# Reordering the fills of a tile in a fused attention kernel: score block first, maximum block second, bias fill ahead of the sums

## The reference

```
x = x + attention(group_norm(x))        # 32 groups, no learned scale
qkv = gn @ qkv_w + qkv_b                # 12 heads of 16 channels, S = 2304 positions
attn = softmax(q k^T / 4 + rel_h[.., row of key] + rel_w[.., column of key])
out = (attn @ v) @ proj_w + proj_b
```

## Time and profile before

| | |
|---|---|
| runs | 6806.47, 6808.59, 6817.65 us; median 6808.59 us |
| profiled execution, first to last instruction | 6801.4 us (no run time of its own was noted for it) |
| TensorE clock granted, mean | 0.996 |
| busy PE / DVE / ACT / POOL | 99% / 80% / 70% / 14% |

### The profile page before, as it was taken

The page is one execution under the profiler, slowest core; times in us unless marked ns, Lnnn a source line. Parts: engine busy times, 40 slices in busy tenths (PEclk is TensorE's granted clock), DMA queues, the critical chain, the costliest instruction groups (busy, mean ns, idle before and its releaser), DMA issues.

```text
span 6801.4 us, 139326 instructions
## 1 busy us (share of the span) xinstructions
PE 6725.5 (99%) x53600; PEld 4245.8 (62%) x53600; DVE 5454.7 (80%) x9973; ACT 4753.7 (70%) x10225; POOL 938.1 (14%) x967
## 2 busy tenths in 40 slices
PE   7999999999999999999999999999999999999998
PEld 5666666666666666666665666666666666666664
DVE  7887888778887788877888778887888878888883
ACT  3776776767767777677776767767676676767775
POOL 2111010211112110121111210102101121101110
PEclk8999999999999999999999999999999999999999
DMA  6676676767677677667676766767677676777673
GB/s 164 148 156 152 137 160 138 163 151 142 152 144 168 144 143 156 149 158 149 142 155 149 158 143 143 161 145 166 140 144 157 147 165 138 143 152 156 144 154 88
DMA packets 306307, 1013.72 MB, mean 149 GB/s; under 512 B 107440, under 2 KB 196976, under 8 KB 215920
## 3 DMA queue, kind: packets, MB, share of 16 engines
q1 hardware_dynamic: 305648, 1004.81, 68.9%
HBM read 745.26 MB, written 255.69 MB: 147 GB/s over the span
## 4 chain that ended last, share of the span: by engine, by line
PE 96%; DMA 1%; DVE 1%; issue 0%; ACT 0%; SPq 0%; POOL 0%; DVEq 0%; ACTq 0%
PE work L805 30%; PE work L878 27%; PE work L796 27%; PE work L824 7%; PE work L843 3%; PE work L862 2%; PE work L851 1%; DMA moving<-rel_scratch 1%; DVE mpart L683 1%; PE work L830 0%; DVE xb L674 0%; ACT probs L561 0%; DMA back<-attention_scratch 0%; DVE hi L721 0%; PE work L835 0%
## 5 line engine op out<-in xcount | busy, mean ns | idle before, releaser
L683 DVE TENSOR_REDUCE mpart<-work 128x1 f32<-128x512 f32 (+1 forms) x8640 | 5088.7, 632 | 1079.7 <-PE work L805 1013.1
L561 ACT ACTIVATE probs<-work 128x512 f32<-128x512 f32 (+1 forms) x8640 | 4100.2, 564 | 866.6 <-PE work L796 852.1
L805 PE MATMUL work<-mkeys,hi 128*128 128x512 f32 (+1 forms) x8640 | 3404.1, 395 | 10.6 <-DVE mpart L683 8.8
L796 PE MATMUL work<-moving,keys 113*128 113x512 f32 (+1 forms) x8640 | 3299.9, 383 | 10.9 <-DMA moving<-rel_scratch 5.7
L805 PEld LDWEIGHTS work<-mkeys,hi 128*128 128x128 f32 x8640 | 1643.6, 190 | 622.4 <-DVE mpart L683 324.0
L878 PE MATMUL work<-probs,vall 128*17 128x288 f32 x27648 | 2013.1, 409 | 0.0
L796 PEld LDWEIGHTS work<-moving,keys 113*128 113x128 f32 x8640 | 1642.1, 190 | 362.3 <-ACT probs L561 39.2
L878 PEld LDWEIGHTS work<-probs,vall 128*17 128x17 f32 x27648 | 637.3, 96 | 846.8 <-ACT probs L561 358.3
L824 PEld LDWEIGHTS work<-image,tab 128*48 128x48 f32 x6912 | 401.6, 124 | 544.9 <-ACT probs L561 513.2
L490 POOL TENSOR_TENSOR full<-full,hi 128x384 f32<-128x384 f32 x576 | 583.5, 1016 | 938.7 <-DVE hi L721 937.6
L495 POOL TENSOR_TENSOR rden<-oraw,rden 128x576 f32<-128x576 f32 x96 | 137.1, 1428 | 3955.3 <-DMA rden<-inverse_scratch 3955.3
(11 more groups left out here) (42 smaller groups left out, 646.8 us busy)
## 6 DMA issues: line engine op xcount, KB each, us to landing
moving<-rel_scratch SPq DMA_DIRECT2D x1728, 144.0 KB
moving<-qk_scratch SPq DMA_DIRECT2D x288, 576.0 KB
rel_scratch<-hi SPq DMA_DIRECT2D x192, 432.0 KB, 5.7
rel_scratch<-full SPq DMA_DIRECT2D x192, 432.0 KB, 5.5
moving<-rel_scratch SPq DMA_DIRECT2D x288, 288.0 KB
image<-qk_scratch SPq DMA_DIRECT2D x384, 144.0 KB, 3.2
keys<-qk_scratch SPq DMA_DIRECT2D x192, 288.0 KB, 7.8
qk_scratch<-split_hi SPq DMA_DIRECT2D x144, 192.0 KB, 3.9
```

Of the source, the lines that this page charges most:

```text
L561: act.activation(probs[:, tile % RING, lo:up], bank[:, 0:up - lo], ACT.Exp).then_inc(act_read, 1)
L683: dve.tensor_reduce(mpart[:, u % 2, q, m:m + 1], bank[:, 0:MSPLIT[m][1] - MSPLIT[m][0]], AX.X, ALU.max)\
L796: pe.matmul(bank[:, 0:up - lo], tile_of(keys[0:K_ROWS, u % 2, :], c, third), moving[0:K_ROWS, slot_of(u, third)[0], lo:up], start=True, st ...
L805: pe.matmul(bank[:, 0:up - lo], hi[:, u % 2, q * P:(q + 1) * P], mkeys[:, u % 2, lo:up], start=True, stop=True).then_inc(for_dve, 1)
```

## The change

The score block goes ahead of the plan's items of a step. The score order becomes short block first, the maximum order short block last. The bias fill goes from the head of step 0 to step 5, where the items now go ahead of the sums. ACT's order and the numbering in `counts()` follow. No instruction is added or removed. One tile's order on PE is then: score(256) max(512) score(512) max score max score max score(512) max(256) [rel], then the sums.

```diff
-SPLIT = [(512 * i, min(512 * i + 512, N)) for i in range(5)]
+MSPLIT = [(512 * i, min(512 * i + 512, N)) for i in range(5)]
+SPLIT = MSPLIT[-1:] + MSPLIT[:-1]
 SB = len(SPLIT)
-MSPLIT = SPLIT[-1:] + SPLIT[:-1]
...
             if t < 12 and u + 2 < UNITS:
-                plan[u][t][0].insert(0, ("rel", u + 2, t))
+                plan[u][t][SB].append(("rel", u + 2, t))
...
                 if 0 <= u < UNITS and i < SB:
-                    items.append(("score", TILES * u + t, i))
+                    items.insert(0, ("score", TILES * u + t, i))
...
                     for i in range(SB + 1):
+                        if 0 <= u < UNITS and i < SB:
+                            consume(("score", TILES * u + t, i))
                         for item in plan[u][t][i]:
                             if item[0] in ON_ACT:
                                 consume(item)
-                        if 0 <= u < UNITS and i < SB:
-                            consume(("score", TILES * u + t, i))
...
                     for i in range(SB + 1):
+                        if 0 <= u < UNITS and i < SB:
+                            fill(("score", tile, i))
+                        for item in plan[u][t][i]:
+                            fill(item)
                         if i == SB and 0 < tile <= TILES * UNITS:
                             attend(tile - 1)
-                        for item in plan[u][t][i]:
-                            fill(item)
-                        if 0 <= u < UNITS and i < SB:
-                            fill(("score", tile, i))
```

## The result

The changed kernel took 6832.66 us (median of 6 runs, 6829.57 to 6834.45) against 6811.73 us for the kernel before in the same runs: a ratio of 1.003, 95% interval 1.0019 to 1.0041. So it is 0.3% slower, 21 us by the medians. The forecast was 6847 us, slower by 38 us, range 6797 to 6900.

What follows compares the result with a forecast made beforehand. The prediction took PE to be the bound, 99% busy and 96% of the chain. Its terms 18 + 10 + 11 - 3 + 2 = +38 us on a span of 6801.4, plus 7.2 us, gave 6847 us, range 6797 to 6900.

Steps and rivals of the forecast that it cites:

- the seams: PE empties on entering and leaving the sums; new order priced 0.68 against 0.67 us (eight bias matmuls), 0.51 against 0.49 (four).
- rival B: Sums' load need not wait behind the bias fill: 0.12 us less in 1152 tiles, -138 us, 6709; chance 0.12.
- rival C: Maximum ahead of the bias fill must empty first: 0.11 to 0.13 us more in 1152 tiles, 6985; chance 0.04.
- The order on ScalarE's ring: In tile 1 of 67 units, the bias fill waits for an exponential delayed by copies of the sums: +10 us.
- Statistics units: In 42 tiles of seven units, `bn_stats` delays the read that the short maximum waits for: 0.26 us each, +11 us.
- The order on VectorE's ring: In about 1230 tiles the last, short maximum waits for the second long one's read: 0.015 us each, +18 us.
- The rest: Scores-only tiles at the end gain, -3 us in 22 tiles; waits for `moving` at a tile's first score grow, +2 us.
- More waits for `moving`: Sign of being wrong: more waits for `moving` than the 21 counted before, at a tile's first score.
- The base: Span of 6801.4 us before the change, with 7.2 us added between span and median to reach the forecast time.
- Rival A: No change: loads' spare time swallows the late reads; 0 to +13 us, 6809 to 6822; chance 0.15.
- D: Rival: VectorE's reads are the new bound, each ordinary tile loses 0.075 us: +75 us in all, 6920; chance 0.09.

Runs made afterwards that it cites:

- e1: Changed kernel with the second of ScalarE's two copies of the sums, in tile 1 of a unit, one step later: 6814.34 us.
- e2: Changed kernel with VectorE's `bn_stats` in the seven statistics units one step later: 6816.94 us.
- e9: Changed kernel with the maximum order short block first as well: 6813.90 us.
- e7: Changed kernel without the loads of bias rows for tiles 3 to 17 of a unit (part of the bias wrong): 6819.28 us.
- e8: Kernel before without the loads of bias rows for tiles 3 to 17 of a unit (part of the bias wrong): 6793.25 us.

## Why the prediction was right, and where it was not

- *PE is the bound, and the seams cost the same.* Right. The sums behind a bias fill take 1.10 (rival B would have shown less), the bias fill behind a maximum 0.35 and 0.19 (rival C: 0.47 and 0.31). Four matmuls came out as priced, eight 0.01 cheaper. On both sides of the sums the load starts 0.07 before the matmuls ahead end; at the bias fill's other side, behind a maximum, it starts 0.01 after the maximum does. So 48 columns of weights behave here as 128 do. The Trainium skill (TensorEngine Tiling (Array Packing), Key Properties) says that a change of tiling mode drains TensorE. The trace agrees with that if the sums, with 17 columns of weights, are the only ones in a mode of their own, which no row here tells. In the prices of B and C the 1152 tiles include 24 bias fills of the start, which have no sums beside them: with the 1128 of the units B is -135, not -138.
- *The order on ScalarE's ring, +10 us.* Right in place and size: 10.0 in 67 tiles, 65 of them with a bias fill that waits 0.26 as forecast (0.27); e1 takes the wait out.
- *Statistics units, +11 us.* Right: 11.1; e2 takes most of it out, e9 the part that comes from the order of the maximum.
- *The order on VectorE's ring, +18 us.* The mechanism is seen in the trace (load 0.14 late, released by the second read) and in e9, the size was off: 8.8 us over the three groups, 7.9 with the loads of rows left out (e7 against e8). The failing step is "So the short maximum ends at 1.88 + 0.05 + 0.39 = 2.32, not 2.31: 0.01 to 0.02 late, I take 0.015". It ends 0.008 late (0.124 instead of 0.116 behind the last long score, by the median), and e9 gives back 0.003 to 0.005 of that. The step took a difference of hundredths from rows printed in hundredths, over 1230 tiles; and the 0.01 that eight bias matmuls save pays part of it.
- *The rest, -3 and +2.* -4.2 in 22 tiles, +1.6 elsewhere. More waits for `moving` was named as a sign of being wrong: they came on the list of waits and not in the time (e7 and e8).
- *The base.* 5 us of the forecast's distance come from the 7.2 us laid around the span; 1.8 was right.

Forecast on spans +38, measured +28.0, and +21 by the medians. Rival A, 0 to +13 us, lies below the measured time, though its upper end touches the interval's lower end; B, C and D did not come.

## What to carry to other kernels

With a ring of three buffers, a new order on the producer moves every wait by some places: write down, for each item, who reads the buffer three places ahead, and when that reader gets to it in the *rare* tiles too, where it has other work. Here 109 rare tiles of 1728 carried three quarters of the loss, and two one-step moves on the reader's side turned 21 us lost into 9 won. Before moving a copy, look on both sides of it: what it delays on its own engine, and what it frees.

## What the runs showed of the hardware that was not expected

- A long list of waits need not be lost time. The first score of a tile, now right behind the sums, shows 43.5 us of waits for `moving`, of which taking all these loads away gives back no more than in the kernel before (13 against 16 us). The trace shows why: nearly every first load behind the sums has 0.48 us of idle time ahead of it, listed as "issue" (817.0 us, 1768 times), and 24 of the 42 loads that are put down to `moving` start at just that point. The other 18 start later than it by 12 us in all (the 11 of before by 6.5), and the 11.1 us of the 18 matmuls behind them are the same waits once more.
- Two blocks of 256 columns in a row, each with a weight load of 0.19 us, follow without loss that shows: behind the sums the short score takes 0.32 and the short maximum 0.12 (e9).
- The profiled span and the time of the same execution lie 1.7 to 1.9 us apart in every run where both are known; one execution of a kernel to the next differs by up to 18 us here, about as much as the change itself, so small changes were read from paired tiles.
